# A four-layer graph network on one Trainium2 core: last features in two buffers, a projection copied by transfers, all queues in a new order

## What is computed

```
layer 0: H = xW; a = softmax(leaky(s_i + t_j), edges only); relu(a H)
layer 1: 8 heads of 16: h = xW; a = softmax(leaky(s_i + t_j), edges only); elu(a h)
layer 2: (mean over the edges' neighbours of x) W1 + x Ws^T + b; layernorm * gamma + beta; relu
layer 3: 4 heads of 32: w = xW; a = softmax(w_i . w_j / sqrt(32), edges only); a w
```

## Time and profile before

| | us |
|---|---|
| median of 3 runs | 2634.27 |
| lowest, highest | 2633.69, 2635.55 |
| profiled execution: span | 2633.3 |
| its own time | given by its span alone |
| PE, DVE, ACT, POOL busy | 2370.0, 2178.8, 1961.1, 156.0 |

### The profile page before, as it was taken

One profiled execution on the slowest core, in us unless ns is written; L12 is line 12 of the kernel. 1 busy time (PEld: TensorE's weight loads), 2 busy tenths in 40 slices (PEclk: granted clock), 3 DMA queues, 4 the chain that ended last, 5 costly groups with the idle time before them and its releaser, 6 DMA issues.

```text
span 2633.3 us, 56947 instructions
## 1 busy us (share of the span) xinstructions
PE 2370.0 (90%) x23877; PEld 1568.4 (60%) x23877; DVE 2178.8 (83%) x4097; ACT 1961.1 (74%) x2193; POOL 156.0 (6%) x104
## 2 busy tenths in 40 slices
PE   3668998999999999999989899999989999998966
PEld 3658565575756557575655757556575755657331
DVE  3689798897979889798888979788897978989656
ACT  2748787777879777787977778787777878777724
POOL 0000000000000000000000000000000000000000
PEclk9779999999999899999999999999999999999978
DMA  5504041221414223041322304032130403101000
GB/s 124 121 25 122 25 113 42 73 74 34 97 33 98 57 65 81 15 116 33 90 65 58 89 9 122 33 82 73 47 98 11 122 33 82 41 26 42 9 1 17
DMA packets 190417, 164.42 MB, mean 62 GB/s; under 512 B 136656, under 2 KB 170576, under 8 KB 189136
## 3 DMA queue, kind: packets, MB, share of 16 engines
q1 hardware_dynamic: 188864, 127.22, 17.3%
q0 software_dynamic: 1296, 33.56, 6.3%
HBM read 151.78 MB, written 42.53 MB: 74 GB/s over the span
## 4 chain that ended last, share of the span: by engine, by line
PE 46%; DVE 28%; ACT 14%; issue 10%; DMA 1%; SPq 1%; POOL 0%; ACTq 0%; POOLq 0%; DVEq 0%
PE kp L783 13%; PE kp L766 9%; ACT ramp L959 9%; PE fp L605 9%; DVE weight L1290 8%; PE kp L759 6%; PE fp L666 4%; ACT weight L1006 3%; DVE bstat L1098 2%; DVE vh L1298 2%; PE fp L559 1%; PE fp L552 1%; DVE yb L1364 1%; PE fp L684 1%; DVE weight L1427 1%
## 5 line engine op out<-in xcount | busy, mean ns | idle before, releaser
L959 ACT ACTIVATE ramp<-s1row,tbig 128x1024 bf16<-128x1024 f32 x864 | 922.6, 1145 | 72.6 <-DVE weight L1290 70.4
L1006 ACT ACTIVATE weight<-kp,shift 128x1024 f32<-128x1024 f32 x512 | 545.7, 1110 | 271.4 <-PE kp L766 269.9
L1290 DVE TENSOR_TENSOR weight<-ramp,AT 128x2048 bf16<-128x2048 bf16 x512 | 612.3, 1220 | 106.6 <-ACT ramp L959 61.3
L666 PE MATMUL fp<-vh_parts,weight 128*128 128x102 bf16 x8192 | 457.2, 215 | 88.8 <-DVE weight L1290 58.6
L666 PEld LDWEIGHTS fp<-vh_parts,weight 128*128 128x128 bf16 x8192 | 413.8, 101 | 190.5 <-DVE weight L1290 95.7
L783 PE MATMUL kp<-weight,w 128*33 128x512 f32 x2048 | 489.0, 600 | 11.4 <-DVE weight L1427 10.9
L766 PE MATMUL kp<-shared 32*128 32x512 f32 x2048 | 299.7, 655 | 7.9 <-ACT weight L1006 7.5
L783 PEld LDWEIGHTS kp<-weight,w 128*33 128x33 f32 x2048 | 97.8, 110 | 313.2 <-issue 247.4
L605 PEld LDWEIGHTS fp<-h,weight 128*128 128x128 f32 x2048 | 234.5, 194 | 40.0 <-issue 27.8
L605 PE MATMUL fp<-h,weight 128*128 128x129 f32 x2048 | 240.3, 279 | 16.2 <-DVE weight L1203 16.2
L1427 DVE SCALAR_TENSOR_TENSOR weight<-AT,weight 128x1024 f32<-128x1024 bf16 x182 | 214.6, 1221 | 44.2 <-ACT weight L1006 44.2
(11 more groups left out here) (184 smaller groups left out, 2575.9 us busy)
## 6 DMA issues: line engine op xcount, KB each, us to landing
s1row<-s_rows_dram SPq DMA_DIRECT2D x128, 512.0 KB, 4.2
adj_bf_dram<-in_adj_dram POOLq DMA_DIRECT2D x15, 2048.0 KB, 13.3
x<-in_x_dram SPq DMA_DIRECT2D x16, 512.0 KB, 7.2
xfT<-s_row_dram SPq DMA_DIRECT2D x16, 512.0 KB, 5.6
out_dram<-elu SPq DMA_DIRECT2D x16, 512.0 KB, 3.2
adj_bf_dram<-in_adj_dram POOLq DMA_DIRECT2D x2, 1024.0 KB, 10.3
s_rows_dram<-weight SPq DMA_DIRECT2D x16, 32.0 KB
AT<-adj_bf_dram SPq DMA_TRANSPOSE x17, 10.9
```

The lines of the kernel that those rows point to most:

```text
L666: last = pe.matmul(fp[:, 1 + t // 4, col:col + 2 * PARTS * C1], edges[:, u % B_RING, t * P:(t + 1) * P], vh_parts[:, jt, h, :, :, :].rearr ...
L959: act.activation(ramp[:, u % R_RING, :], s1row[:, h % S_RING, :], ACT.Relu, bias=tbig1[:, jt, h:h + 1], scale=BIG).then_inc(ramp_ready.sem, 1)
L1006: act.activation(weight3[:, w % P_RING, :], kp[:, 1 + 2 * (w % 2):3 + 2 * (w % 2), :].rearrange("p a n -> p (a n)"), ACT.Exp, bias=shift3[ ...
L1290: dve.tensor_tensor(edges[:, u % B_RING:u % B_RING + 2, :], ramp[:, u % R_RING:u % R_RING + 2, :], AT[:, third, jt:jt + 2, :], ALU.min).th ...
```

## The change

1. x3 has two buffers, chosen by the batch's parity.
2. `h0` and `h1`, the projected features of layers 0 and 1, lie in one buffer `features`. Their columns of ones, set once before, are now set in each batch (`layer0_top`, `layer0_finish`).
3. `rhs3_far`, the far matmuls and their two copies on ACT are gone. SP copies the two halves of the partitions of `wT[:, 0]` crosswise into `wT[:, 1]` by two transfers (`spread_far`), and the first scores wait for them (`far_loaded`).
4. All tables are new, SP and POOL have one too. `prepare_rest` and the turning of the self weights have steps of their own. `schedule` is written for several sections, but all periods use the one table.

The diff, cut to its core (the `step` functions issue the same calls as the `period` functions did, under the new tables):

```diff
-        rhs3_far = sb("rhs3_far", [P, D])
...
         v0neg = sb("v0neg", [P, T])
-        h0 = sb("h0", [P, T, D + 1])
+        features = sb("features", [P, T * H1 * C1])
+        h0 = features[:, 0:T * (D + 1)].rearrange("p (t d) -> p t d", t=T)
+        h1 = features[:].rearrange("p (t h c) -> p t h c", t=T, h=H1)
...
         x1 = sb("x1", [P, T, D])
-        h1 = sb("h1", [P, T, H1, C1])
...
         y2_hi = sb("y2_hi", [P, T, D + 1], BF16)
-        x3 = sb("x3", [P, T, D])
+        x3 = sb("x3", [P, 2, T, D])
...
         shift_ready = signal("shift_ready", 1)
-        wT_made = signal("wT_made", 2)
-        wT_ready = signal("wT_ready", 2)
+        wT_made = signal("wT_made", 1)
+        wT_ready = signal("wT_ready", 1)
+        far_loaded = signal("far_loaded", 32)
...
 
-        def schedule(period):
+        def schedule(tables, step):
 
             def there(b):
                 return b if 0 <= b < NB else None
-            for f in range(-1, NB + 2):
-                period(f % 3, there(f), there(f - 1), there(f - 2), there(f + 1))
-
-        STEPS = 444
+            for stage, periods in zip(STAGE, SECTIONS):
+                for s in range(STEPS):
+                    for at, f in zip(tables[stage], periods):
+                        step(s, at, f % 3, there(f), there(f - 1), there(f - 2), there(f + 1))
...
+        STEPS = 109
+        ON_PE = [
+            (dict(maxima1=93, maxima3=44, project0=[25, 31, 35], project1=91, project2=102, project3=42, scores3=[49,
+                 53, 56, 60, 65, 71, 75, 83, 85, 87, 90, 94, 98, 101, 104, 106], self2=0, self_weights=62, shift3=47,
+                 sources1=95, spread0=48, spread1=96, sum1=[17, 18, 23, 26, 28, 30, 37, 38], sum2=[1, 2, 5, 8, 9, 11,
+                 15, 16], top0=40, turn0=[19, 24], turn1=89, turn2=99, turn3=39, turn_back=29, unit0=[73, 74, 77, 78,
+                 79, 80, 81, 82], unit1=[3, 4, 6, 7, 10, 12, 13, 14, 20, 21, 22, 27, 32, 33, 34, 36, 41, 43, 45, 46,
+                 50, 51, 52, 55, 58, 59, 63, 64, 66, 67, 68, 70], values3=[54, 57, 61, 69, 72, 76, 84, 86, 88, 92, 97,
+                 100, 103, 105, 107, 108]),),
+        ]
+        ON_ACT = [
+            (dict(cut1=[81, 85], cut1_second=[86, 90], elu=66, exp3=[31, 32, 35, 36, 38, 39, 42, 43, 47, 48, 52, 53,
+                 58, 61, 62, 63, 64, 65, 68, 69, 71, 72, 74, 75, 78, 79, 83, 84, 88, 89, 92, 93], exps0=34, exps1=77,
+                 first2=87, out3=[49, 67, 82, 96], prepare0=46, project0=[15, 18, 21], project1=73, project3=26,
+                 ramps=[0, 1, -1, 2, 3, 4, -1, 5, 6, 8, 9, 11, 13, 14, 16, 17, 22, 23, 28, -1, 29, 30, -1, 33, 37, -1,
+                 40, 41, 44, 45], ramps_ahead=[94, 95], second2=91, self2=7, sources1=76, sum1=[19, 20, 24],
+                 turn0=[10, 12], turn1=70, turn2=80, turn3=25, unit0=[50, 51, 54, 55, 56, 57, 59, 60], wide3=27),),
+        ]
+        ON_DVE = [
+            (dict(affine2=19, columns1=[92, 94], cut1=[95, 97], cut1_third=[102, 103], divide1=82, elu1=85,
+                 finish0=83, finish1=73, finish3=24, head1=[7, 13, 22, 29, 40, 49, 56, 65], lengths3=34, low2=101,
+                 mask3=33, masked3=[57, 62, 63, 64, 69, 70, 71, 72, 80, 81, 86, 91, 93, 96, 99, 100], maxima1=88,
+                 maxima3=36, maximum0=45, most0=35, norm0=84, norm1=89, norm3=27, out2=15, prepare=74, ramps=[2, 9,
+                 37, 44, 52], relu2=21, residual3=50, rest2=98, shift0=58, shift3=38, shifts1=90, stats2=16, tail3=61,
+                 top0=28, top1=87, unit0=[66, 67, 68, 75, 76, 77, 78, 79], unit1=[0, 1, 3, 4, 5, 6, 8, 10, 11, 12, 14,
+                 17, 18, 20, 23, 25, 26, 30, 31, 32, 39, 41, 42, 43, 47, 48, 51, 53, 54, 55, 59, 60], z0=46),),
+        ]
+        ON_POOL = [
+            (dict(adjacency=3, rstd0=4, rstd1=5, rstd2=0, rstd3=1, rstd_tail=2),),
+        ]
+        ON_SP = [
+            (dict(adjacency=1, far=6, out=10, sources=[2, 3, 4, 5, 7], sources_ahead=[12, 13, 14], spread_row=9,
+                 store_row=8, store_sources=11, x=0),),
...
-            def period(r, f, k, m, n):
-                if n is not None and n > 0:
+            def spread_far(b):
+
+                sp.wait_ge(wT_ready.sem, wT_ready.of(b))
+                for side in range(2):
+                    sp.dma_start(wT[(1 - side) * P // 2:(2 - side) * P // 2, 1, :],
+                                 wT[side * P // 2:(side + 1) * P // 2, 0, :]).then_inc(far_loaded.sem, 16)
+
+            def store_out(b):
+                sp.wait_ge(x4_ready.sem, x4_ready.of(b))
+                sp.dma_start(rows(out, b), x4[:]).then_inc(stored.sem, 16)
+
+            def step(s, at, r, f, k, m, n):
+                if n is not None and n > 0 and s == at["x"]:
                     load_x(n)
+                if n is not None and n > 0 and s == at["adjacency"]:
                     turn_adjacency(n, (r + 1) % 3)
+                if n is not None and s == at["store_row"]:
+                    store_row(n)
+                if n is not None and s == at["spread_row"]:
+                    spread_row(n)
                 for h in range(S_RING, H1):
-                    if n is not None and h == ROW_AT:
-                        store_row(n)
-                    if f is not None:
+                    if f is not None and s == at["sources"][h - S_RING]:
                         spread_sources(f, h)
-                    if n is not None and h == ROW_AT:
-                        spread_row(n)
-                if m is not None:
-                    sp.wait_ge(x4_ready.sem, x4_ready.of(m))
-                    sp.dma_start(rows(out, m), x4[:]).then_inc(stored.sem, 16)
-                if n is not None:
+                if k is not None and s == at["far"]:
+                    spread_far(k)
+                if m is not None and s == at["out"]:
+                    store_out(m)
+                if n is not None and s == at["store_sources"]:
                     store_sources(n)
-                    for h in range(S_RING):
+                for h in range(S_RING):
+                    if n is not None and s == at["sources_ahead"][h]:
                         spread_sources(n, h)
 
-            schedule(period)
...
                 if o3_ready.any_before(b):
                     pe.wait_ge(o3_ready.sem, o3_ready.before(b))
-                turn_rows(x3, kp_pair, x3_turned)
+                turn_rows(x3[:, b % 2], kp_pair, x3_turned)
 
             def layer3_project(b, f):
                 pe.wait_ge(x3T_ready.sem, x3T_ready.of(b))
@@ -727,13 +768,9 @@
                     last = pe.matmul(kp[:, 3 + t // 4, (t % 4) * D:(t % 4 + 1) * D], x3T[:, t * P:(t + 1) * P],
                                      rhs3[:], start=True, stop=True)
                 last.then_inc(w3_made.sem, 1)
-                for bank, weights, n in ((0, rhs3, 0), (1, rhs3, 1), (2, rhs3_far, 0)):
-                    last = pe.matmul(kp[:, bank, :], weights[:], x3T[:, n * HALF:(n + 1) * HALF], start=True, stop=True)
+                for n in range(2):
+                    last = pe.matmul(kp[:, n, :], rhs3[:], x3T[:, n * HALF:(n + 1) * HALF], start=True, stop=True)
                 last.then_inc(wT_made.sem, 1)
-
-            def layer3_project_rest(b):
-                pe.wait_ge(wT_ready.sem, wT_ready.of(b, 1))
-                pe.matmul(kp[:, 0, :], rhs3_far[:], x3T[:, HALF:N], start=True, stop=True).then_inc(wT_made.sem, 1)
 
             def layer3_turn_maxima(b):
                 pe.wait_ge(qmax_ready.sem, qmax_ready.of(b))
@@ -750,6 +787,7 @@
                 if v == 0:
                     pe.wait_ge(mask3_made.sem, mask3_made.of(b))
                     pe.wait_ge(wT_ready.sem, wT_ready.of(b))
+                    pe.wait_ge(far_loaded.sem, far_loaded.of(b))
                     pe.wait_ge(shift_ready.sem, shift_ready.of(b))
                 for w in (2 * v, 2 * v + 1):
                     _, n, J = unit3(w)
...
 
-            def layer3_wide(b, x):
-                act.wait_ge(wT_made.sem, wT_made.of(b, x + 1))
-                if x == 0:
-                    copy(wT[:, 0, :], kp_pair).then_inc(wT_ready.sem, 1)
-                    copy(wT[:, 1, 0:HALF], kp[:, 2, :])
-                else:
-                    copy(wT[:, 1, HALF:N], kp[:, 0, :]).then_inc(wT_ready.sem, 1)
+            def layer3_wide(b):
+                act.wait_ge(wT_made.sem, wT_made.of(b))
+                copy(wT[:, 0, :], kp_pair).then_inc(wT_ready.sem, 1)
 
...
@@ -1171,6 +1195,7 @@
 
             def layer0_top(b):
                 dve.wait_ge(h0_ready.sem, h0_ready.of(b))
+                dve.memset(h0[:, :, D:D + 1], 1.0)
                 dve.tensor_reduce(st0[:, 32:33], st0[:, T:2 * T], AX_X, ALU.max).then_inc(tmax0_ready.sem, 1)
 
             def layer0_topmost(b):
@@ -1204,7 +1229,9 @@
                                          op1=ALU.mult).then_inc(weight0_ready.sem, 1)
 
             def layer0_finish(b):
+                front.begin(b)
                 dve.wait_ge(weight0_used.sem, weight0_used.of(b))
```

(5 more changed lines are left out.)

542 lines of the change are left out of this document (257 added, 285 removed).

## The result

The changed kernel takes **2536.87 us** (median of 4 runs, 2532.39 to 2537.89) against 2633.98 us beside it (4 runs): a ratio of 0.963, 95% interval 0.961 to 0.964. I had forecast 2583 us and a range of 2548 to 2616.

A forecast was written before the change was run, and what follows sets the result against it. It took PE to bound a period's last 89 us and DVE the 45 us before. From 2634.3 us, -54 (3.6 us in 15 periods), +1.7 lead-in and +0.6 last batch gave 2583 us; range 2548 to 2616 us.

The forecast's parts named there:

- The residual's move: Residual goes from before the third normalisation to behind pair 25, so x3 is turned earlier: 3.9 us a period gained.
- The turning to the scores: From x3's turning to the first scores, DVE's chain shortens and the scores follow its shift at 12.3 us: 1.8 us gained.
- I cost the transfers at nothing: The crosswise copy lands 11.6 us behind the turning, covered by DVE's chain to the shift, scores at 12.3 us: no cost.
- The estimate of 3.2 us: The Trainium skill's fit for both crosswise transfers, quoted beside the 4.5 us that the forecast used; it would give 2581 us.
- I take back 1.4 us: a new order brings waits of its own: Deduction from the period's -5.0 us for new waits and DVE's higher load beside PE's stretch, leaving -3.6 us.
- the pair that moved in: One pair's matmuls come behind the scores' start instead of before the turning, into PE's stretch: +0.7 us a period.
- The lead-in: At the kernel's start, DVE's preparing of the other weights now stands between units 2 and 3 of layer 0: +1.7 us.
- The end: Last batch: 1.9 us gained by the residual, 2.5 us lost to transfers that nothing covers: +0.6 us together.
- twice the 1.4 us taken back: Stated reason, with some clock, for the range's lower end of 2548 us.
- Nearly all waits go: Rival: 3 us of PE's idling left in the three stretches, 7 us a period gained: 2530 us, chance 0.08.
- PE's work only: Rival: new order brings as many waits as it ends, only PE's 2.07 us a batch gained: 2601 us, chance 0.25.
- The transfers come late: Rival: PE stands at the first scores until landing, slower than before beyond 17.3 us after the turning: 2658 us, chance 0.09.

The follow-up runs named there:

- no. 5: Changed kernel with layer 3's residual early, ahead of the third normalisation, and POOL's adjacency fetch behind layer 0's root: 2591.72 us, ratio 0.985.
- no. 2: New code in the old orders, with only layer 3's residual and tail moved later (behind pairs 25 and 31): 2625.15 us, ratio 0.997.
- no. 4: Changed kernel with the crosswise copy made in batch 0 only, later batches awaiting no transfer (computation incomplete): 2520.68 us, ratio 0.957.
- no. 7: Changed kernel with a semaphore for each half of the crosswise copy, awaited behind the mask's matmuls and at unit 8: 2521.33 us, ratio 0.958.
- no. 11: Changed kernel with the old order of ACT and DVE at the end of a period: 2544.86 us, ratio 0.967.
- no. 13: Changed kernel with the old order on PE, ACT and DVE from a period's start to layer 3's shift, residual still late: 2572.99 us, ratio 0.977.
- no. 16: The kernel of no. 13 plus 17 idle matmuls a period in three of TensorE's waits: 2538.98 us, ratio 0.964.
- no. 6: Changed kernel with the far projection back on TensorE and its two copies back on ACT: 2535.65 us, ratio 0.963.
- no. 1: The changed code with the tables and queue orders of the kernel before, residual still early: 2642.52 us, ratio 1.003.
- no. 10: Changed kernel with TensorE's old order of scores, values and pairs in the scores stage: 2619.22 us, ratio 0.995.
- no. 9: Changed kernel with TensorE's old order of column sums, layer 0's turnings and the projection's pieces in the first half: 2730.06 us, ratio 1.036.
- no. 17: The kernel of no. 1 plus idle matmuls in two of TensorE's waits, 6 ahead of pair 14 and 5 ahead of the maxima: 2639.42 us, ratio 1.002.
- no. 15: As no. 9, column sums late on TensorE, but layer 0's turnings and the projection's pieces early enough for ACT: 2696.9 us, ratio 1.024.
- no. 12: The kernel of no. 7 with only pair 18 moved ahead of layer 3's maxima on TensorE: 2520.3 us, ratio 0.957.
- no. 3: Changed kernel with the residual and its statistics early, right ahead of the third normalisation: 2652.25 us, ratio 1.007.

## Why the prediction was wrong in size

**The residual's move** was right in mechanism and somewhat too large in its stretch. I forecast 3.9 us from the degrees to the turning, where the measured stage lost 3.1; no. 5 puts the price of the residual at 3.8 us a period, 2.6 in that stretch and 0.9 in the next. It needs the other orders around it: in the old ones the same move gave 17 us and not 55 (no. 2).

**The turning to the scores**: forecast -1.8 us, measured -1.9 (-2.1 with the missing mask). That they agree is luck, for the parts changed. The transfers were sized well: ACT's copy ended 7.0 us behind the turning (7.1 forecast), and the second half landed at 11.5 us (11.6 forecast), 4.4 us after the first issue (4.5 forecast). DVE's chain was not: its shift was ready at 10.5 us, and I had the scores follow it at 12.3. The cover that I named ended 0.9 us before the transfers landed, and "I cost the transfers at nothing" was wrong by the 1.0 us a batch that no. 4 and no. 7 get back. The estimate of 3.2 us from the Trainium skill (DMA: Bandwidth & Descriptors, Anatomy of one DMA) would have hidden them. The page fits it to transfers that GpSimd issues, and SP issues these; the trace has a median of 3.5 us for one of the two and 4.4 for both. The single transfer over 128 partitions, which the prediction quotes as the advice, was not tried.

**The failed step is "I take back 1.4 us: a new order brings waits of its own"**, with the stages that I gave nothing or a loss. The new orders brought no waits on balance. TensorE's waits of over 0.15 us, summed over the eleven periods of each trace, went from 7.8 to 6.8 us a period, and from 10.7 to 8.5 in number. And the clock, which I had read in the earlier trace rows and used in one rival only, belonged in the sum:
- The scores stage: forecast +0.7 us for the pair that moved in, measured -0.4 to -0.6. Its waits did not shrink (0.7 us a period before, 0.9 after). What shrank is the loss to the lower clock, (1 - clock) times the length: 1.4 us before, 0.4 after. Before, the four masks at its start ran slow in all eleven periods (the earlier trace rows have 1.72 us for them), and in the changed kernel in one of eleven.
- The stretch ahead of the degrees: costed at nothing, measured -1.4 us; no. 11 finds 1.1 of it in the order of ACT and DVE at the period's end.
- The first half: I had argued only with the residual. The old order on three engines costs 36 us there (no. 13), and idle work alone gave 34 us of that back (no. 16). So what this order buys is TensorE's clock.

By stage the misses are -1.4, +0.8, -0.1 and -1.3 us, and -1.4 for the taking back: 3.4 us a period, where a steady one lost 7.0 and 3.6 was forecast. Over the 15 intervals, of which the last is short and gained only 3.2 us, 97 us were gained and 54 forecast: 43 us of the error of 46. (I had also read the period as 152.6 us; that mean takes in the short last interval, a steady one has 154.9.) The small terms erred against each other. The lead-in gained 4.1 us where I forecast 1.7 us of loss. The end cost 3.7 us where I forecast 0.6: the copy cost the 2.5 us that I gave it (81.0 us from the last shift on, 78.5 in nos. 4 and 6), but the 1.9 us of gain beside it came as 1.2 us of loss.

The range was drawn too narrow by its own reason as well: "twice the 1.4 us taken back" is 42 us below the forecast, 2541 us, and not 2548. The 2537 us would still lie below it.

**The rivals.** *Nearly all waits go* (2530 us, 0.08) is nearest to what came, and in part by its own reason, "the clock comes back where PE no longer idles"; but most of the waits stayed (6.8 of 7.8 us a period). *PE's work only* fell with the time itself and with no. 1: in the old order the two matmuls less gained nothing. In the new one they and ACT's two copies are worth some 15 us (no. 6 against nos. 4 and 7), not 33, and the wait for the copy takes them back. *The transfers come late*: PE's wait at the first scores does end with the landing, which I had named as a sign of being wrong, but at 11.9 us at the latest, far from the 17.3 us at which it decides.

**What the clock is worth.** By the table, (1 - clock) times the stage's length is 2.0 + 1.3 + 1.4 = 4.7 us a period before and 0.7 + 0 + 0.4 = 1.2 after. Of the last stage, where TensorE is the bound, that is 1.0 us a period of the 7.0. In the other stages it counts only where TensorE is the late one, and how much that is I can't say from these runs.

**What stays open.** Which part of the change brought how much is not settled. The parts don't add. Put back alone, the residual costs 55 us, the first half 36, the scores stage 59 and the period's end 8: 158 us where the change is worth 97. Orders taken back on one engine alone cost still more (82 us in no. 10, 193 in no. 9). Any split of the 97 us depends on the order in which the parts are taken. The first of the changes, the two buffers of x3, is what allows the late residual; the shared buffer of the features was in every run and has no price of its own.

## What to carry to other kernels

- A wait on TensorE in a stage that another engine bounds isn't free if the next stage is TensorE's: price it with the granted clock at the start of that stage. Where such waits can't be removed, idle matmuls into a free bank are a cheap test, and here a remedy: 17 of them a period brought back 34 us of the whole (no. 16). Filling two waits of several brought back 3 us (no. 17).
- The order of one queue is right or wrong only against the others'. Judge or undo a reordering on all engines at once, and test a wait that you take for the cause: the longest new one of no. 9, 242 us on ACT, was gone in no. 15, and 160 of the 193 us lost were still there.
- When a transfer's landing is what a stage waits for, first place the wait where the data is read, with a semaphore for each part. That took 16 us off the changed kernel (no. 7: 2521.33 us; with no. 12 the fastest that compute everything).

## What the hardware showed that I had not expected

- Two issues of a copy within SBUF took SP up to 5.8 us and not 1.1, and one landed in 6.2 us and not 3.5 in the median, when POOL's 2 MB fetch from DRAM to DRAM was under way (no. 3); with that fetch later it was 3.6 us again (no. 5). No row of the kernel before shows it, as that kernel has no such copy. It cost 60 us, about as much as the part of the change under test.
- Behind waits of 1.2 and 1.9 us, with TensorE partly at work between them, its clock was at the lower level: four matmuls of 128x512 took 1.86 us for 1.02 (no. 13 against no. 16). The Trainium skill (TensorE: Matmul & The Clock Gate, What's actually happening) calls the lower clock the default and has activity release it; no. 16 agrees, as idle matmuls alone raised the granted clock from 0.937 to 1.000 ahead of the scores.
